# Attention's value sums: denominators divided out through DMA hops instead of by turning, and two half units joined into one

## What is computed

```python
# x: (4, 2048, 256); 16 heads of 16
q, k, v = heads(ln(x) @ w_q.T), heads(ln(x) @ w_k.T), heads(ln(x) @ w_v.T)
scores = q @ k.T / 4, masked: causal, but the first 196 positions see each other
ctx = softmax(scores) @ v                     # heads side by side: (4, 2048, 256)
x = x + ln(ctx @ w_o.T + b_o)
# mixture of experts: 8 experts, best 2 per token, plus a shared one
x = x + ln(moe(ln(x)))
```

## Time and profile before

| | us |
|---|---|
| median of 3 runs | 2268.48 (2265.04 to 2271.96) |
| the profiled execution | 2254.69 |
| its span | 2253.0 |
| PE busy | 2077.8 (92%) |
| ACT busy | 1701.5 (76%) |
| DVE busy | 1477.8 (66%) |
| POOL busy | 647.4 (29%) |

### The profile page before, as it was taken

One profiled execution on the slowest core, in us unless ns is written; L12 is line 12 of the kernel. 1 busy time (PEld: TensorE's weight loads), 2 busy tenths in 40 slices (PEclk: granted clock), 3 DMA queues, 4 the chain that ended last, 5 costly groups with the idle time before them and its releaser, 6 DMA issues. The chain is left out here.

```text
span 2253.0 us, 38463 instructions
## 1 busy us (share of the span) xinstructions
PE 2077.8 (92%) x14097; PEld 1272.1 (56%) x14097; DVE 1477.8 (66%) x2384; ACT 1701.5 (76%) x2165; POOL 647.4 (29%) x645
## 2 busy tenths in 40 slices
PE   7995999999999999999999696999999999999980
PEld 6773333333333333333333686888888888888870
DVE  5663256455556565555565697777788888888877
ACT  5663999999999999999999475333466666666656
POOL 1111000000000000000000353777145565566546
PEclk9996999999999999999999897999999999999995
DMA  6887655555444455554330684574467776677667
GB/s 219 309 296 188 121 69 77 77 74 68 59 59 59 67 77 77 74 74 58 58 59 8 198 289 160 193 259 161 171 204 207 180 181 171 171 172 198 155 180 285
DMA packets 161574, 324.37 MB, mean 144 GB/s; under 512 B 18000, under 2 KB 91856, under 8 KB 155632
## 3 DMA queue, kind: packets, MB, share of 16 engines
q1 hardware_dynamic: 128820, 268.13, 46.2%
q0 software_dynamic: 30256, 46.03, 11.2%
q10 hardware_dynamic: 2316, 7.80, 1.0%
HBM read 198.75 MB, written 127.47 MB: 145 GB/s over the span
## 5 line engine op out<-in xcount | busy, mean ns | idle before, releaser
L1112 ACT ACTIVATE att_prob<-att_scores 128x1024 f32<-128x1024 f32 (+2 forms) x1122 | 1001.3, 1013 | 54.0 <-PE att_scores L1059 49.2
L1078 PE MATMUL att_out<-att_prob,att_va 128*32 128x512 f32 (+3 forms) x5000 | 577.6, 543 | 18.3 <-DVE att_prob L1144 18.2
L1059 PEld LDWEIGHTS att_scores<-att_qs,att_ks 50*128 50x128 f32 x2560 | 209.2, 185 | 486.2 <-ACT att_prob L1112 397.4
L1059 PE MATMUL att_scores<-att_qs,att_ks 50*128 50x512 f32 (+3 forms) x2560 | 458.7, 428 | 21.1 <-PEq L118 17.2
L1830 POOL DMA_INDIRECT sums<-moe_y,moe_token x142 | 307.7, 2167 | 252.1 <-ACT moe_y L2111 207.9
L1144 DVE SCALAR_TENSOR_TENSOR att_prob<-att_prob,att_tri 128x512 f32<-128x512 f32 x224 | 144.7, 687 | 295.5 <-ACT att_prob L1112 295.5
L1010 POOL DMA_DIRECT2D ctx_scr<-att_cout x64 | 48.7, 760 | 987.1 <-DVE att_cout L1194 948.0
L1078 PEld LDWEIGHTS att_out<-att_prob,att_va 128*32 128x32 f32 x5000 | 109.8, 108 | 193.2 <-ACT att_prob L1112 90.0
L1981 PE MATMUL moe_ps<-moe_xt_hi,w_first_hi 128*128 128x512 f32 (+1 forms) x448 | 175.6, 392 | 3.5 <-ACT moe_h L2084 2.2
L1981 PE MATMUL moe_ps<-moe_xt_lo,w_first_hi 128*128 128x512 f32 (+1 forms) x448 | 172.2, 384 | 0.0
L1981 PE MATMUL moe_ps<-moe_xt_hi,w_first_lo 128*128 128x512 f32 (+1 forms) x448 | 172.0, 384 | 0.0
(11 more groups left out here) (295 smaller groups left out, 3901.7 us busy)
## 6 DMA issues: line engine op xcount, KB each, us to landing
qk_parts<-proj_qk SPq DMA_DIRECT2D x64, 512.0 KB, 4.6
keep_first_weights<-w_experts SPq DMA_DIRECT2D x22, 1412.0 KB, 6.6
moe_wraw<-w_experts SPq DMA_DIRECT2D x21, 1412.0 KB, 6.6
att_qs<-qk_parts SPq DMA_DIRECT2D x180, 128.0 KB
att_ks<-qk_parts SPq DMA_DIRECT2D x180, 128.0 KB
moe_rows<-rows_in SPq DMA_DIRECT2D x23, 544.0 KB, 3.8
proj_xin<-x SPq DMA_DIRECT2D x16, 512.0 KB, 3.8
v_scr<-proj_va SPq DMA_DIRECT2D x16, 512.0 KB, 3.5
```

What stands on the lines that cost most here:

```text
L1059: last = nc.tensor.matmul(pss[e % SBUFS][:, h, at:at + CH - q0], ks[s][rows, half, kt * P:(kt + 1) * P], qs[s][rows, half, c * CH + q0:(c ...
L1078: last = nc.tensor.matmul(pso[k % 2][strip, q0:], va[team % 2][:, kt, strip], probs_of(u)[:, h, at:at + CH - q0], start=(kt == 0), stop=(i ...
L1112: nc.scalar.activation(probs_of(u)[:, half * 2:half * 2 + 2, start:], pss[e % SBUFS][:, :, start:], ACT.Exp, scale=HD ** -0.5)\
```

## The change

It does four things.

1. The sums are no longer turned. The value columns come first in each head's 32 columns and the other 16 are ones, so that each head's strip of 32 partitions has 16 rows of sums and 16 rows that all hold the denominator. DVE's copy writes the queries in the order in which `attention_out` wants them, into one of three buffers `osb`. The denominators (4 rows of 512) then go over DMA: SP moves them to a tile of 32 x 64 (`move_denominators`); DVE inverts it six steps after the copy (`invert`); POOL stores it to DRAM, waits, loads it back as 128 x 512, waits, multiplies `osb` and stores the context with the features on the rows (`ctx_rows`).
2. A copy into `osb` waits until the context of three blocks before has been stored.
3. In `attention_out` the context is loaded already turned, by two DMAs, so that the eight transposes of each chunk are gone. The very last block is inverted, spread, multiplied and stored inside `attention_out`, by DVE, ACT and POOL at steps 3 to 7, and its chunk is the last.
4. The half units of c = 1 and c = 2 become one full unit, placed behind the first unit of c = 2. A team has 35 units.

```diff
+def load_features(eng, to, rows, done):
+    teams = TEAMS // KT
+    for k in range(KT):
+        each = rows[k * teams:(k + 1) * teams].rearrange("a (h r) t -> (a h) r t", r=VA_W)
+        eng.dma_start(to[:, k], each[:, 0:HD]).then_inc(done, 16)
...
+PAIRED = 1
 def units():
+    def narrowest(c):
+        return TPC * c + 2, 2 * P, c
     for c in range(BCH):
         diagonal = TPC * c
         for kt in range(diagonal):
-            yield c, ((kt, 0, 0),), 0
-        yield c, ((diagonal, 0, 0),), 0
+            yield ((kt, 0, 0, c),), 0
+            if kt == 0 and c == PAIRED + 1:
+                yield tuple((t, q0, at, of) for at, (t, q0, of) in ((0, narrowest(c)), (2 * P, narrowest(PAIRED)))), 0
+        yield ((diagonal, 0, 0, c),), 0
         if c == 0:
             assert P < PREFIX < 2 * P
-            yield c, ((1, 0, 0),), 0
-            yield c, ((2, 2 * P, 2 * P), (3, 3 * P, P)), P
+            yield ((1, 0, 0, c),), 0
+            yield ((2, 2 * P, 2 * P, c), (3, 3 * P, P, c)), P
         else:
-            yield c, ((diagonal + 1, P, P), (diagonal + 3, 3 * P, 0)), 0
-            yield c, ((diagonal + 2, 2 * P, 2 * P),), 2 * P
+            yield ((diagonal + 1, P, P, c), (diagonal + 3, 3 * P, 0, c)), 0
+            if c not in (PAIRED, PAIRED + 1):
+                yield ((diagonal + 2, 2 * P, 2 * P, c),), 2 * P
...
-TURN = VALUES + 1
-FINISH = VALUES + 1
+INVERT = COPY + 6
+OBUFS = 3
...
-LATE_STEPS = {13: 1, 14: 2, 15: 2, 16: 2, 17: 1, 21: 1, 23: 1, 24: 1, 25: 2, 26: 1, 27: 2, 28: 1, 29: 2, 30: 1}
+LATE_STEPS = {13: 1, 14: 2, 15: 2, 16: 2, 17: 1, 20: 1, 22: 1, 23: 1, 24: 2, 25: 1, 26: 2, 27: 1, 28: 2, 29: 1}
...
+        self.osb = [ph.sb(f"osb{i}", [P, CH]) for i in range(OBUFS)]
+        self.dens = ph.sb2("dens", [TEAM * DEN_ROWS, CH // DEN_ROWS])
+        self.shares = ph.sb2("shares", [TEAM * DEN_ROWS, CH // DEN_ROWS])
+        self.inverse = ph.sb2("inverse", [P, CH])
...
+        self.inv_rows = [inv_scr[s].rearrange("h (r t) -> (h r) t", r=DEN_ROWS) for s in range(2)]
+        self.inv_wide = [inv_scr[s].unsqueeze(1).broadcast_to([TEAM, VA_W, CH]) for s in range(2)]
...
-                for team in range(ALL_TEAMS):
-                    for c in range(BCH):
-                        k, at = team * BCH + c, team % TEAMS * TEAM * HD
-                        pool.wait_ge(c_done, k + 1)
-                        pool.dma_start(ctx_ch[team // TEAMS * BCH + c, :, :, at:at + TEAM * HD], cout[k % 2][:])\
-                            .then_inc(stored[k % 2], 16)
-                for s in range(2):
-                    pool.wait_ge(stored[s], ALL_TEAMS * BCH // 2 * 16)
+                for k in range(LAST_K):
+                    n, s = divmod(k, 2)
+                    pool.wait_ge(o.inverted[s], n + 1)
+                    pool.dma_start(o.inv_rows[s], shares[s][:]).then_inc(o.kept[s], 16)
+                    pool.wait_ge(o.kept[s], (n + 1) * 16)
+                    pool.dma_start(inverse[s][:], o.inv_wide[s]).then_inc(o.spread[s], 16)
+                    pool.wait_ge(o.spread[s], (n + 1) * 16)
+                    sums_at = osb[k % OBUFS]
+                    nc.gpsimd.tensor_tensor(sums_at[:], sums_at[:], inverse[s][:], ALU.mult).then_inc(o.c_done, 1)
+                    pool.wait_ge(o.c_done, k + 1)
+                    pool.dma_start(o.place(ctx_rows, k), sums_at[:]).then_inc(o.stored[k % OBUFS], 16)
...
+                def move_denominators(k):
+                    n, s = divmod(k, 2)
+                    sp.wait_ge(o.o_copied, k + 1)
+                    if n:
+                        sp.wait_ge(o.inverted[s], n)
+                    sp.dma_start(dens[s][:], osb[k % OBUFS][HD::VA_W].rearrange("h (r t) -> h r t", r=DEN_ROWS))\
+                        .then_inc(o.moved[s], 16)
                 for team in range(1, ALL_TEAMS):
+                    k = (team - 1) * BCH
                     if team > 1:
+                        move_denominators(k - 1)
                         sp.wait_ge(used, (team - 1) * NU)
-                    load_heads(sp, team, slice(0, BCH), loaded[team % 2])
+                    load_parts(sp, team, slice(0, BCH), loaded[team % 2], 0)
+                    move_denominators(k)
+                    load_parts(sp, team, slice(0, BCH), loaded[team % 2], 1)
+                    load_values(sp, team, slice(0, BCH), loaded[team % 2])
...
+                    for c in range(1, BCH - 1):
+                        move_denominators(k + c)
...
+                        wait_from_one(pe, o.o_copied, k - 1)
...
-                def turn(k):
-                    pe.wait_ge(o_copied, k + 1)
-                    for j in range(TPC):
-                        last = nc.tensor.transpose(pso[k % 2][:, j * P:(j + 1) * P],
-                                                   osb[k % 2][:, j * P:(j + 1) * P], ident[:])
-                    last.then_inc(o_turned, 1)
...
-                    wait_from_one(dve, o_turned, k - 1)
-                    V.tensor_copy(osb[k % 2][:], pso[k % 2][:]).then_inc(o_copied, 1)
+                    wait_from_one(dve, o.stored[k % OBUFS], k // OBUFS * 16)
+                    V.tensor_copy(osb[k % OBUFS][:].rearrange("p (j q) -> p j q", j=TPC),
+                                  pso[k % 2][:].rearrange("p (q j) -> p j q", j=TPC)).then_inc(o.o_copied, 1)
...
-                def finish(k):
-                    dve.wait_ge(o_turned, k + 1)
-                    o = pso[k % 2][:].rearrange("p (g w) -> p g w", w=VA_W)
-                    V.reciprocal(rden[k % 2][:], o[:, :, 0]).then_inc(inverted, 1)
-                    wait_from_one(dve, stored[k % 2], k // 2 * 16)
-                    dve.wait_ge(inverted, k + 1)
-                    V.tensor_tensor(cout[k % 2][:].rearrange("p j (h d) -> p (j h) d", h=TEAM), o[:, :, 1:1 + HD],
-                                    rden[k % 2][:].unsqueeze(2).broadcast_to([P, TPC * TEAM, HD]),
-                                    ALU.mult).then_inc(c_done, 1)
+                def invert(k):
+                    n, s = divmod(k, 2)
+                    dve.wait_ge(o.moved[s], (n + 1) * 16)
+                    if n:
+                        dve.wait_ge(o.kept[s], n * 16)
+                    V.reciprocal(shares[s][:], dens[s][:]).then_inc(o.inverted[s], 1)
...
+                for r in range(len(RING_UNITS) + INVERT):
+                    if r >= INVERT and end_of.get(RING_UNITS[r - INVERT], LAST_K) < LAST_K:
+                        invert(end_of[RING_UNITS[r - INVERT]])
...
-                        sp.wait_ge(c_turned, c - 1)
-                    sp.dma_start(cin[c % 2][:], ctx_ch[c]).then_inc(c_loaded[c % 2], 16)
+                        sp.wait_ge(c_lo, c - 1)
+                    if c == NCH - 1:
+                        sp.wait_ge(o.stored[LAST_K % OBUFS], o.stores_to(LAST_K, LAST_K % OBUFS) * 16)
+                    load_features(sp, cin[c % 2], ctx_rows[c], c_loaded[c % 2])
...
-                def turn(c):
-                    if c == 0:
-                        pe.wait_ge(first_loaded, 2 * 16)
-                    else:
-                        pe.wait_ge(c_loaded[c % 2], (c + 1) // 2 * 16)
-                    if c:
-                        pe.wait_ge(c_lo, c)
-                    transposes(nc, psT, cin[c % 2], ident).then_inc(c_turned, 1)
...
-                    act.wait_ge(c_turned, c + 1)
+                    if c == 0:
+                        act.wait_ge(first_loaded, (FEATURE_LOADS + 1) * 16)
+                    else:
+                        act.wait_ge(c_loaded[c % 2], (c + 1) // 2 * FEATURE_LOADS * 16)
                     if c >= 2:
                         act.wait_ge(o_done, 2 * (c - 1))
-                    nc.scalar.activation(ct[c % 2][0][:], psT[:], ACT.Copy).then_inc(c_hi, 1)
+                    nc.scalar.activation(ct[c % 2][0][:], cin[c % 2][:], ACT.Copy).then_inc(c_hi, 1)
...
-                    V.tensor_tensor(ct[c % 2][1][:], psT[:], ct[c % 2][0][:].bitcast(F32), ALU.subtract)\
+                    V.tensor_tensor(ct[c % 2][1][:], cin[c % 2][:], ct[c % 2][0][:].bitcast(F32), ALU.subtract)\
```

146 lines of the change are left out of this document (89 added, 57 removed).

## The result

The changed kernel takes 2334.06 us (median of 4 runs, 2331.95 to 2339.81) where the kernel before took 2269.03: ratio 1.030, 95% interval 1.028 to 1.032. It is slower by 65 us; the forecast was faster by 20.

| us | before | before again | changed |
|---|---|---|---|
| attend | 1033.6 | 1034.0 | 1104.0 |
| of it the first team | 71.1 | 71.2 | 85.6 |
| of it teams 1 to 14, mean | 64.18 | 64.20 | 68.23 |
| to attention_out's first low part | 11.6 | 11.6 | 5.8 |
| its 16 low parts, first to last | 114.6 | 117.6 | 125.1 |

A forecast was written before the change was run, and what follows sets the result against it. PE and ACT were taken to bound attend, DVE attention_out. Terms -19.2 - 12 + 14.7 + 2 - 4 - 2 + 0.5 = -20 us took 2268.5 to 2248 us; range 2231 to 2268, with 2 us more below.

The forecast's parts named there:

- The half units: Attend, ends of c = 1 and c = 2: joining them saves 1.20 us a team, 19.2 us in all.
- the first paragraph of the prediction: What bounds the kernel: in attend PE and ACT both look full; DVE bounds attention_out.
- The turns: Attend: without PE's turns of blocks, 0.8 us a team less for 15 teams, 12 us.
- The first team: Attend's first team: ACT waits for block 0's and block 1's moved denominators, 5.1 and 9.6 us, together +14.7.
- the first sum: First team, block 0: move lands at 236, then reciprocal, masks, values and scores; ACT starts at 239.4, cost 5.1 us.
- Steady teams: Attend's later teams: waits for moves and stores cost nothing, except block 1's 0.15 us a team; +2 us.
- The times after zero: Steady team, from c = 3's copy: block 0's move near 16, block 1's 32 to 33, store landing 35 to 38.
- The second rival: Attend: every team waits, ACT losing 1 to 2 us in each of 14 teams; 2268, chance 0.17.
- The barrier and the first turn: Between attend and attention_out: no store landing before the barrier, -4 us; no first turn in the stage, -2 us.
- attention_out: That stage: DVE still takes 7.64 us a chunk; POOL's multiplication for the last block may delay one chunk, +0.5 us.
- The fourth rival: attention_out: with less work PE's clock falls to the low level in most of the stage; 2283, slower; chance 0.07.
- The signs named as making the forecast wrong: Team above 63 us, DVE's waits ending ACT's idle time in every team, or low parts over 8 us apart.

The follow-up runs named there:

- kernel j: h with the half units of c = 1 and c = 2 left apart; 2268.43 us, ratio 0.9989 to the kernel before.
- n: k with the half units of c = 1 and c = 2 left apart; 2264.52 us, ratio 0.9963 to the kernel before.
- k: h with eight unread transposes a chunk put back on PE in attention_out; 2254.81 us, ratio 0.9923 to the kernel before.
- h: The changed kernel with later reciprocals and SP's query and key loads issued three at a time; 2267.22 us, ratio 0.9981 to the kernel before.
- d: The changed kernel with eight unread transposes a chunk put back on PE in attention_out; 2315.16 us, ratio 1.0266 to the kernel before.

## Why the prediction was wrong, point by point

- **The half units, -19.2 us.** Wrong: 0 in the kernel before, 0.1 to 0.2% within a round in the cured one. The step that failed is taking the joined stretch by itself. It did take 5.43 us; but PE, which the first paragraph of the prediction had at 1013 of 1036 us, then stood for two score buffers at the late unit's scores, and the three units there took 7.44 us in place of 6.17. What makes the buffers late stays open.
- **The turns, -12 us.** Half at the most. The first three units of a team went from 5.79 to 5.30 us, as said; the whole team from 64.2 to 63.8 in kernel j, and in n, whose attend is the same, it took 64.2 (one team of 67.7 among them). So 0 to 0.4 of the 0.8 us.
- **The first team, +14.7 us.** 14.5 measured, and the agreement is luck: ACT stood 8.3 and 5.2 us where I had 5.1 and 9.6, with the reciprocals at 238.1 and 259.8, and the two errors nearly cancel. (By its own terms the first sum gives 239.1 and not 239.4, so 4.8 and 9.9; the total stays.)
- **Steady teams, +2 us.** This is the term that failed: it has both moves land before DVE's next masks are due, and prices them at nothing for block 0 and 0.15 us a team for block 1. What came in its place: DVE waited for moved denominators 27 times, 4.5 us each, and ACT stood 4.6 us a team longer than before. A team takes 68.2 us; the forecast's 62.2 and the measured one are 6 us apart, 84 us in 14 teams, of which a part is the missing gain above (1.6 us a team) and the rest, over 4 us, waits. The times after zero were each a little late: 17.2 against "near 16", 34.7 against "32 to 33", 39.0 for the issue of a store that I had landing at 35 to 38. I had read the end of the burst from a kernel without the hops, added the hops to POOL's clock but not to the DMA engines', and then set tenths of a microsecond of margin against them. The second rival had the mechanism, and its second hop at 35 and copy 4 us late are the 35.3 and 4.0 of the team above; but the cost came at the mask behind block 1's move, which it names last, and at block 0's, and it priced them at 1 to 2 us a team.
- **The barrier and the first turn, -6 us.** 5.8 measured.
- **attention_out, +0.5 us.** +7.5 to +10.5. The fourth rival, with 0.07 of the chances, came true at a quarter of its price: the granted clock fell to 0.84 to 0.87 in the steady part, not to the low level throughout. That the clock is the cause is borne out by k against h and d (7 to 9 us); the other kernels with the transposes gave 3 to 4 us.
- The signs named as making the forecast wrong (a team above 63 us, DVE's waits in every team, low parts more than 8 us apart) all showed: 68.2, 27 waits in 15 teams, 8.34.

## What to carry to other kernels

When a change puts small transfers that someone waits for into a queue that also carries bulk loads, space the bulk out by the consumer's progress before judging anything else; here that alone was worth 70 us, while holding the burst back cost 160. Where two engines are both near full, don't count a saving on one before you have looked at what it waits for a few steps later: here it was lost again four and five units on. And count an added transfer twice, once on the engine that waits for it and once on the queue in which everything else becomes later.
